# Writing out an attention loop and re-dividing one slot's matmul work among its score steps

## The reference

```
q = l2norm(x @ Wq); k = l2norm(x @ Wk); v = x @ Wv; a = sigmoid(x @ Wg)    # 8 heads of 128
for each token t:  S = a_t[:, None] * S + k_t[:, None] * v_t[None, :]      # state 128 x 128 per head
                   o_t = q_t @ S
x = layernorm(x + o @ Wo)
x = layernorm(x + ffn(x))    # two linear + swiglu layers around a mixture of 8 routed and 2 shared experts
```

## Time and profile before

| | |
|---|---|
| median of 3 runs | 2013.74 us (2011.88 to 2014.73) |
| the profiled execution | 2015.12 us, span of its trace 2013.3 us |
| mean granted TensorE clock | 0.96 |
| instructions | 75320 |
| attention, first to last slot's S1 | 32.65 to 1460.09 us of the span |
| ffn part | from about 1490 us to the end |

### The profile page before, as it was taken

One profiled execution on the slowest core, in us unless ns is written; L12 is line 12 of the kernel. 1 busy time (PEld: TensorE's weight loads), 2 busy tenths in 40 slices (PEclk: granted clock), 3 DMA queues, 4 the chain that ended last, 5 costly groups with the idle time before them and its releaser, 6 DMA issues.

```text
span 2013.3 us, 75320 instructions
## 1 busy us (share of the span) xinstructions
PE 1769.1 (88%) x29575; PEld 1411.6 (70%) x29575; DVE 1595.3 (79%) x3391; ACT 1194.5 (59%) x2608; POOL 936.1 (46%) x731
## 2 busy tenths in 40 slices
PE   6998888898888888888988888899879999999997
PEld 5777767777777777677777777677756666666664
DVE  6898779797878787797978787788957778787775
ACT  6766656565656566565656565566635555555553
POOL 6554445454545444454545454445514444444443
PEclk9999989899999999899999999999989999999998
DMA  7000000000000000000000000000000000000000
GB/s 195 8 3 9 3 8 3 8 2 8 8 3 8 3 8 3 8 3 8 2 8 8 3 8 3 8 3 8 3 12 11 11 21 21 10 21 10 21 16 11
DMA packets 28580, 26.13 MB, mean 13 GB/s; under 512 B 1928, under 2 KB 23696, under 8 KB 28304
## 3 DMA queue, kind: packets, MB, share of 16 engines
q1 hardware_dynamic: 28304, 21.77, 3.7%
HBM read 13.38 MB, written 4.19 MB: 9 GB/s over the span
## 4 chain that ended last, share of the span: by engine, by line
PE 42%; issue 22%; DVE 18%; POOL 11%; ACT 5%; DVEq 1%; POOLq 0%; DMA 0%; ACTq 0%; SPq 0%
DVE k_sb L1236 6%; PE bank L674 5%; PE bank L532 5%; PE bank L622 5%; POOL wq_lo L500 4%; POOL wk_lo L500 4%; PE bank L533 4%; PE bank L534 4%; PE bank L664 4%; PE bank L581 3%; PE bank L619 3%; DVE s_sb L1274 3%; PE bank L638 3%; DVE tot_sb L320 2%; PE bank L607 2%
## 5 line engine op out<-in xcount | busy, mean ns | idle before, releaser
L456 POOL TENSOR_TENSOR sq_lo<-sq_sb,sq_hi 128x512 bf16<-128x512 f32 x256 | 330.2, 1290 | 533.3 <-ACT sq_hi L962 532.1
L1236 DVE TENSOR_TENSOR qq_sb<-qq_sb,tot_sb 128x512 f32<-128x512 f32 (+1 forms) x384 | 257.7, 671 | 177.3 <-PE bank L619 173.6
L1236 DVE TENSOR_TENSOR k_sb<-k_sb,tot_sb 128x512 f32<-128x512 f32 (+1 forms) x384 | 379.3, 988 | 3.5 <-PE bank L622 2.2
L461 POOL TENSOR_TENSOR rn_sb<-ss_sb,expo 128x8 f32<-128x8 f32 x128 | 214.8, 1678 | 122.3 <-DVE ss_sb L1281 122.3
L1009 ACT ACTIVATE at_sb<-diag_sb 32x256 f32<-32x256 f32 x256 | 106.0, 414 | 202.7 <-DVE diag_sb L1248 198.0
L984 ACT ACTIVATE v_sb<-bank,rn_sb 128x128 f32<-128x128 f32 x512 | 139.0, 383 | 71.3 <-PE bank L534 68.1
L500 POOL TENSOR_TENSOR wq_lo<-v_sb,wq_hi 128x512 fp32r<-128x512 f32 x80 | 103.7, 1296 | 146.8 <-ACT wq_hi L1132 146.8
L500 POOL TENSOR_TENSOR wk_lo<-v_sb,wk_hi 128x512 fp32r<-128x512 f32 x80 | 104.2, 1302 | 134.0 <-ACT wk_hi L1132 134.0
L619 PEld LDWEIGHTS bank<-qq_sb,k_sb 128*32 128x32 f32 x12288 | 123.9, 110 | 58.7 <-issue 40.9
L664 PE MATMUL bank<-v_sb,at_sb 128*128 128x128 f32 x1024 | 147.5, 287 | 18.2 <-DVE res L1288 18.2
L619 PE MATMUL bank<-qq_sb,k_sb 128*32 128x16 f32 x12288 | 141.6, 185 | 20.8 <-DVE k_sb L1236 12.1
(11 more groups left out here) (204 smaller groups left out, 4820.7 us busy)
## 6 DMA issues: line engine op xcount, KB each, us to landing
x_nat<-in_L_attn_x_dram SPq DMA_DIRECT2D x16, 256.0 KB, 3.8
x_nat<-x_all SPq DMA_DIRECT2D x16, 256.0 KB, 2.4
out_dram<-k_sb SPq DMA_DIRECT2D x16, 256.0 KB, 2.3
ew_raw<-in_L_ffn_exp_w_dram SPq DMA_DIRECT2D x3, 512.0 KB, 5.8
qq_sb<-in_L_attn_Wq_dram SPq DMA_DIRECT2D x1, 512.0 KB, 3.9
qq_sb<-in_L_attn_Wk_dram SPq DMA_DIRECT2D x1, 512.0 KB, 5.9
k_sb<-in_L_attn_Wg_dram SPq DMA_DIRECT2D x1, 512.0 KB, 6.7
k_sb<-in_L_attn_Wv_dram SPq DMA_DIRECT2D x1, 512.0 KB
```

Of the source, the lines that this page charges most:

```text
L456: nc.gpsimd.tensor_tensor(sq_lo[:, n, :], sq_sb[:, n % 2, :], sq_hi[:, n, :], ALU.subtract).then_inc(sq_done, 1)
L461: nc.gpsimd.tensor_tensor(rn_sb[par][:, i, :, :].rearrange("p h c -> p (h c)"), ss_sb[:, i * G:(i + 1) * G], expo[:, 0:G], ALU.pow).then_i ...
L1236: return nc.vector.tensor_tensor(view, view, by, ALU.mult)
```

## The change

The three loops of PE, ACT and DVE and that of POOL over batches 1 to 14 become a Python `for`, so that every body is straight code with constant semaphore counts. SP keeps its loop. Within a slot the order is rewritten on PE, ACT and DVE, and one order serves all four slots. PE's becomes: S1, Tk0, q0, q1, S3, Tk1, k2, SU0, S4, k3, SU1, squares 0, S5, OC0, g4, S6, OS0, squares 1, spread norms, g5, S7, OC1, OS1, values, S0 of the next slot. On DVE the two clamps move one to three levels later, `states` moves from behind level 4 to behind level 5, the two `normalise_q` from ahead of the growth of level 6 to behind it, and `own_products` and `first_growth` from ahead of the wait for scores 7 to behind the growth of level 7. On ACT the second gate is taken only behind the copies of scores 6. POOL's order stays.

```diff
@@ -488,7 +488,7 @@
             norms(0, 0)
             body(0, first=True)
-            with pool.Fori(1, B - 1) as b:
+            for b in range(1, B - 1):
                 body(b)
             body(B - 1, last=True)
             ln_rstd(B - 1)
@@ -734,58 +734,54 @@
                 for p, P, has_prev, has_next in slots(b, first, last):
                     par = p % 2
                     prev_p, next_p = (p - 1) % NP, (p + 1) % NP
+                    prev_b = b if p else b - 1
                     n_x = b + 2 if p == NP - 1 else b + 1
-                    if has_next and p < NP - 1:
-                        project(next_p, P + 1, wq, 0)
                     scores(par, P, 1)
                     if has_prev:
                         transposes_of_k(1 - par, P - 1, 0)
                     if has_next:
-                        if p == NP - 1:
-
-                            pe.wait_ge(xt_evac, n_x)
-                            pe.wait_ge(x_lo, n_x)
-                            project(next_p, P + 1, wq, 0)
-                            transposes_of_k(1 - par, P - 1, 1)
+                        pe.wait_ge(xt_evac, n_x)
+                        pe.wait_ge(x_lo, n_x)
+                        project(next_p, P + 1, wq, 0)
                         project(next_p, P + 1, wq, 1)
-                    if has_prev and not (has_next and p == NP - 1):
+                    scores(par, P, 3)
+                    if has_prev:
                         transposes_of_k(1 - par, P - 1, 1)
                     if has_next:
                         project(next_p, P + 1, wk, 2)
                     if has_prev:
                         state_updates(1 - par, P - 1, 0)
-                    scores(par, P, 3)
+                    scores(par, P, 4)
+                    if has_next:
+                        project(next_p, P + 1, wk, 3)
                     if has_prev:
                         state_updates(1 - par, P - 1, 1)
                     if has_next:
-                        project(next_p, P + 1, wk, 3)
                         sums_of_squares(P + 1, 0, n_x)
-                    scores(par, P, 4)
+                    scores(par, P, 5)
                     if has_prev:
-                        outputs_of_chunk(prev_p, P - 1, b if p else b - 1, 0)
+                        outputs_of_chunk(prev_p, P - 1, prev_b, 0)
                     if has_next:
                         project(next_p, P + 1, wg, 4)
-                        project(next_p, P + 1, wg, 5)
-                    scores(par, P, 5)
+                    scores(par, P, 6)
                     if has_prev:
                         outputs_of_state(prev_p, P - 1, 0)
                     if has_next:
                         sums_of_squares(P + 1, 1, n_x)
                         spread_norms(1 - par, P + 1)
-                    scores(par, P, 6)
+                        project(next_p, P + 1, wg, 5)
+                    scores(par, P, 7)
                     if has_prev:
-                        outputs(prev_p, P - 1, b if p else b - 1, 1)
+                        outputs(prev_p, P - 1, prev_b, 1)
                     if has_next:
                         project_values(next_p, P + 1, 0)
                         project_values(next_p, P + 1, 1)
-                    scores(par, P, 7)
-                    if has_next:
                         scores(1 - par, P + 1, 0)
                     if p == NP - 2 and not last:
                         transposes_of_x(b + 1)
             body(0, first=True)
-            with pe.Fori(1, B - 1) as b:
+            for b in range(1, B - 1):
                 body(b)
             body(B - 1, last=True)
             P = B * NP - 1
@@ -961,16 +957,15 @@
                 nc.scalar.activation(sq_sb[:, n % 2, :], src, ACT.Square).then_inc(sq_full, 1)
                 nc.scalar.activation(sq_hi[:, n, :], src, ACT.Square).then_inc(sq_top, 1)
-            def take_gate(par, P):
-                for h in range(HP):
-                    act.wait_ge(pj_full, P * 8 + 5 + h)
-                    if h == 0:
-
-                        await_count(act, q1_done, (P - 1) * 3)
-                        await_count(act, k_up, (P - 1) * 6)
-                        await_count(act, tot_pool, (P - 1) * 2)
-                        await_count(act, tot_done, (P - 1) * 5)
-                    nc.scalar.activation(a_sb[par][:, h * T:(h + 1) * T], pj[h][:, :], ACT.Sigmoid).then_inc(pj_evac, 1)
+            def take_gate(par, P, h):
+                act.wait_ge(pj_full, P * 8 + 5 + h)
+                if h == 0:
+
+                    await_count(act, q1_done, (P - 1) * 3)
+                    await_count(act, k_up, (P - 1) * 6)
+                    await_count(act, tot_pool, (P - 1) * 2)
+                    await_count(act, tot_done, (P - 1) * 5)
+                nc.scalar.activation(a_sb[par][:, h * T:(h + 1) * T], pj[h][:, :], ACT.Sigmoid).then_inc(pj_evac, 1)
             def take_values(par, P, n):
@@ -1043,7 +1038,8 @@
                 nc.scalar.activation(wvo[0][:, n * 4 * D:(n + 1) * 4 * D], fold_ps[n][:, :], ACT.Copy).then_inc(w_hi, 1)
             act.wait_ge(fold_pe, 7)
             nc.scalar.activation(swf[0][:, :], sc[0][:, :], ACT.Copy).then_inc(w_hi, 1)
-            take_gate(0, 0)
+            for h in range(HP):
+                take_gate(0, 0, h)
             for n in range(2):
                 take_values(0, 0, n)
@@ -1056,40 +1052,39 @@
             def body(b, first=False, last=False):
                 for p, P, has_prev, has_next in slots(b, first, last):
                     par = p % 2
-                    if has_prev and p == NP - 1:
+                    if has_prev:
                         take_kT(P - 1, 0)
                     if has_next:
                         take_tile(1 - par, P + 1, 0)
-                    if has_prev:
-                        take_kT(P - 1, 1 if p == NP - 1 else 0)
-                    if has_next:
                         square(1 - par, P + 1, 0)
                         take_tile(1 - par, P + 1, 1)
-                    if has_prev and p < NP - 1:
+                    if has_prev:
                         take_kT(P - 1, 1)
                     if has_next:
                         square(1 - par, P + 1, 1)
                         take_tile(1 - par, P + 1, 2)
                         square(1 - par, P + 1, 2)
+                        take_tile(1 - par, P + 1, 3)
                     if has_prev:
                         first_states(P - 1)
                     if has_next:
-                        take_tile(1 - par, P + 1, 3)
                         square(1 - par, P + 1, 3)
-                        take_gate(1 - par, P + 1)
+                        take_gate(1 - par, P + 1, 0)
                     spread_diagonal(par, P)
                     take_scores_32(par, P)
                     if has_next:
+                        take_gate(1 - par, P + 1, 1)
+                    take_scores_64(par, P)
+                    if has_next:
                         take_values(1 - par, P + 1, 0)
                         take_values(1 - par, P + 1, 1)
-                    take_scores_64(par, P)
                     if p == NP - 2 and not last:
                         take_xT(b + 1)
                     if first and p < 3:
                         high_experts(p)
             body(0, first=True)
-            with act.Fori(1, B - 1) as b:
+            for b in range(1, B - 1):
                 body(b)
             body(B - 1, last=True)
             for h in range(HP):
@@ -1374,15 +1369,13 @@
                     grow(par, 2, "k").then_inc(k_up, 1)
                     keep_level(2, merged(par)[:, :, 1, :])
                     for j in range(3, 7):
-                        if j == 6 and has_next:
-                            for h in range(HP):
-                                normalise_q(1 - par, P + 1, h)
-
                         if j == 3:
                             dve.wait_ge(tot_pool, P * 2 + 2)
                         else:
                             dve.wait_ge(tot_done, P * 5 + j - 3)
+                        if j == 5 and has_next:
+                            clamp_sums(P + 1, 0)
                         dve.wait_ge(qk_full, qk + j)
                         if j < 6:
@@ -1394,36 +1387,35 @@
                             for n in range(j - 1, j if j < 5 else 7):
                                 block_product(dve, nc.vector, par, P, n)
-                        if j == 3 and has_next:
-                            clamp_sums(P + 1, 0)
-                        if j == 4 and has_prev:
+                        if j == 5 and has_prev:
                             states(1 - par, P - 1)
                         if j == 3 and p == 1 and not first:
                             dve.wait_ge(av_done, b * NP * HP)
                             ln_halves(b - 1, y3, x_rows(b - 1))
                         if j == 3 and first and p > 0:
                             low_experts(p - 1)
```

(15 more changed lines are left out.)

## The result

The changed kernel takes 2085.65 us (median of 4 runs, 2081.55 to 2092.42), the kernel before 2013.26 us. The ratio is 1.0363, 95% interval 1.0333 to 1.0392. The forecast was 2060 us and the way it went, slower, was forecast too. Nothing of the ffn part moved: between the first slot's scores 1 and the last slot's the traces differ by 1505.8 - 1427.4 = 78.4 us, and their spans by 77.3 us.

A forecast was written before the change was run, and what follows sets the result against it. Bound: a chain alternating between engines, plus issue time at loop jumps. A 23.4 us slot against 22.66 us, over 63 slots, adds 47 us to 2015 us: 2062 us profiled, 2060 us median; range 1905 to 2150 us.

The forecast's parts named there:

- Straight code: Batch loops of the attention part: removing 13 jumps back at 7.1 us each takes 92 us off.
- The slot's walk: One slot of the new order, scores 1 to next scores 1: 23.0 us, 23.4 us with layer norm and transposed x.
- Steps 1 to 6: Within a slot: S3 at 2.62, S4 5.83, S5 9.4, states' end 14.2, S7 17.3, next S1 23.0 us.
- step 3: S4 to S5: POOL's second pass holds the growth about 0.4 us more; S5 starts at 9.4 us.
- late gate: Second gate projected behind the spread norms: g5 takes 0.79 us before S7; POOL's gate products stall growths 0.6 and 0.45 us.
- step 6: S7 to next S1: own products and first growths stand behind level 7, with gate-product stalls; next S1 at 23.0 us.
- step 4: S5 to the states' end at 14.2 us: PE idle from about 12.4 us, as outputs of state wait for the states.
- the layer norm and the transposed x: Additions by slot of a batch: second 0.85 us, third 0.2 us, fourth 0.4 us; 0.36 us on the mean slot.
- Rival A: POOL's stalls fall into DVE's waits for PE; two passes hidden give a 21.4 us slot, 1936 us; chance 0.29.
- Rival B: PE's idle time lowers the clock in every slot, 1.3 us a slot, 2144 us; chance 0.20.
- Rival C: Instructions cannot come fast enough for 14 straight bodies, so the 92 us stay: 2154 us; chance 0.03.
- Rival D: POOL's powers hold DVE off too, 1.2 and 1.6 us, adding 2.8 us a slot: 2238 us; chance 0.02.

## Why the prediction was right

**Straight code.** Right in kind, and a little small: 92 us forecast, 106.5 us measured with the old order. The straight slots at the end, from which the 85.1 us were read, held a third slot at a granted clock of 0.92 (21.91 us); in straight code twelve of 14 third slots run at 1.00 and take 20.64 us, and the mean of four slots is 83.9 us. The 1.91 us of the torn block were only the smaller of two holes, but the cost was read as a difference of whole turns and so held them both.

**The slot's walk.** Steps 1 to 6 held within 0.3 us each in a first slot at a granted clock of 1.00, and so did the places of the stalls, but for the 0.4 us of the second pass (step 3): 0.1 us of it is seen, and a longer S4 made up for most of the rest. The prices are in part confirmed. For the late gate the walk has 0.79 + 0.6 + 0.45 = 1.8 us a slot; 102 / 63 = 1.6 us were measured, and 1.3 us at a clock of 1.00. PE waits for the states as forecast, but taking this wait away exposes POOL's power and fourth pass, which the walk had right at its side and which I had not priced as next in line. "The whole of it from step 6 and the idle time of PE in step 4" fits the runs but for the layer norm: taking back the gate, the tail, the states, the layer norm (34 us by itself) and the clamp gives 168 of 179 us. The stalls of POOL's passes are dear, 176 us, but the old order has most of them too.

**The layer norm and the clock.** Here the forecast was low. I gave the layer norm and the transposed x 0.36 us on the mean slot, and had it that the layer norm adds only 0.2 us to the third slot. The third slot takes 1.84 us more than the second (24.71 against 22.87 us), the fourth 1.23 us more (24.10 us), the first 0.83 us more (23.70 us). In the third, two passes of POOL lie on the layer norm, 1.7 us, and the clock falls in the leg to S7. In the first and the fourth it is the clock that the sum left out: the seven and six slots at 0.93 are 1.4 and 1.7 us longer than their like at 1.00, 20 us in all. The second slot's layer norm, for which I had 0.85 us, is paid for by luck. Two lines of DVE and one of POOL in the slot from 441.14 us:

```profile
448.65 0.68 DVE L1231 TENSOR_TENSOR qq_sb<-qq_sb,tot_sb 128x512 f32<-128x512 f32 x1
...
453.46 0.59 DVE L320 TENSOR_TENSOR tot_sb<-tot_sb 128x32 f32<-128x32 f32 x3
```

```profile
454.20 1.15 POOL L456 TENSOR_TENSOR sq_lo<-sq_sb,sq_hi 128x512 bf16<-128x512 f32 x1
```

The growth behind S4 (446.92 us) starts 1.73 us after it instead of 1.09 us, and S5 comes 0.5 us later. But the clamp and with it POOL's power and fourth pass come later too, and the pass misses the three gate products, which take 0.59 us instead of 1.48 us. By the third slot's layer norm and the clock the 23.4 us of the forecast became 23.90 us, 63 x 0.5 = 32 us. The 106.5 us of the jumps don't enter, as the sum went from the looped kernel's total straight to the new slot.

**Rival A** did not happen: two to four instructions of DVE are held up by more than 0.6 us in each slot of batches 1 to 14. In 13 of 14 second slots they are two, as A had it, and such a slot still takes 22.7 us, as a rule. **Rival B** happened in part: 26 of the 56 slots of these batches ran at a granted clock of 0.93 or less. The same 1.7 us of idle time at a first slot left the clock at 1.00 in seven batches and not in seven, and what decides between them is not shown. With the states early or the gates early the first slots all stay at 1.00. **Rival C** is excluded by the old order in straight code. **Rival D** is wrong as I put it, since the powers hold no growth, but the reverse is seen: the growths hold a power, 2.62 us instead of 1.64 us, and through it the fourth pass. That fits the rule of the Trainium skill (SBUF — State Buffer, Who interferes with whom) that the order of issue decides which of the two blocks. For the power the traces show only the side on which POOL waits: two growths of 0.69 us (428.43 and 429.03 us) that were issued behind one of 1.64 us (428.09 us) ran inside it unhindered.

## What to carry to other kernels

In a chain that alternates between two engines, lay one period out step by step with the durations of the profile, and put work behind a step only if the other engine is waiting anyway. A removed wait is worth only the distance to the one that ends next: the states' wait was 1.7 us long and gave 0.8 us, part of it through the clock. Ask of work that seems dear in the new kernel what it cost in the old one, before calling it the cause. And two changes in one diff can have opposite signs, here -106 and +179 us, so run them apart.

## What had not been expected

- A TENSOR_SCALAR of 128x128 with one wide SBUF operand, 0.33 us by itself, was held up to 1193 ns by POOL's passes.
- A power on 128x8 elements on POOL took 1.64 us in one place (428.09 us of the changed kernel) and 2.62 us in another (366.81 us with the states early), where a growth of DVE had been issued just before it.
- A jump back of a hardware loop cost 8.2 us in one order of the body, with two holes of PE of 2.93 and 1.91 us and a granted clock of 0.50 behind them, and 4.0 us in another, with holes of 2.62 and 2.19 us.
- A third slot took 22.19 us at a granted clock of 1.00 in the looped new order and 25.13 us at 0.93 in the changed kernel, with the same instructions of the slot. The difference is shared between the clock and one more stall of the layer norm.
- Seven first slots of the changed kernel ran at a granted clock of 1.00 and seven at 0.93, 1.4 us longer, with the same order and the same wait of PE.
